# Decoder on one core: TensorE turns the identity matrix into an unread bank at the heads of stages and ahead of the last output projections

## The reference, cut to what matters

```python
x = _layernorm(x + _L0_attn_ref(x, ...))            # 16 heads of 128, rope             -> stage a
x = _layernorm(x + _L0_xattn_ref(x, ctx_1024, ...)) # 32 heads of 16, axial rope        -> stage b
x = _layernorm(x + _L0_ffn_ref(x, ...))             # 32 experts of 80 rows, top 4 of 3 groups, and a shared one
x = _layernorm(x + _L1_attn_ref(x, ...))            # 16 heads of 32, causal            -> stage d
x = _layernorm(x + _L1_xattn_ref(x, ctx_1024, ...)) # 16 heads of 128, rms-normed q, k  -> stage e
x = _layernorm(x + _L1_ffn_ref(x, ...))             # 8 experts, top 2
```

```python
q = x @ Wq; k = s @ Wk; v = s @ Wv        # s is x itself, or the context
w = softmax(q @ k.T * scale)
return (w @ v) @ Wo
```

## Time and profile before

| | us |
|---|---|
| median of 3 runs (lowest, highest) | 3435.64 (3432.76, 3437.16) |
| the profiled execution's own time | 3431.57 |
| its span | 3429.8 |
| PE busy | 3125.4 (91%) |
| DVE busy | 2102.3 (61%) |
| POOL busy | 1478.2 (43%) |
| ACT busy | 1293.4 (38%) |

### The profile page before, as it was taken

One profiled execution on the slowest core, in us unless ns is written; L12 is line 12 of the kernel. 1 busy time (PEld: TensorE's weight loads), 2 busy tenths in 40 slices (PEclk: granted clock), 3 DMA queues, 4 the chain that ended last, 5 costly groups with the idle time before them and its releaser, 6 DMA issues. The chain is left out here.

```text
span 3429.8 us, 58056 instructions
## 1 busy us (share of the span) xinstructions
PE 3125.4 (91%) x20720; PEld 2611.0 (76%) x20720; DVE 2102.3 (61%) x3794; ACT 1293.4 (38%) x3291; POOL 1478.2 (43%) x1470
## 2 busy tenths in 40 slices
PE   7999999999969999899896999699999999969991
PEld 5887878878857777678674777488888888759991
DVE  5666566676636767621185777566667677745566
ACT  3343333333336666401222333244444444324440
POOL 4554343444422343310163222255555556545565
PEclk9999999999989999889997999799999999979996
DMA  4001016022310111149574112210101001147665
GB/s 175 16 13 57 0 36 235 0 79 104 141 48 26 48 34 62 69 164 339 173 166 123 37 40 65 98 60 25 47 12 48 11 24 38 47 172 242 238 228 159
DMA packets 137869, 317.13 MB, mean 92 GB/s; under 512 B 18425, under 2 KB 30457, under 8 KB 135538
## 3 DMA queue, kind: packets, MB, share of 16 engines
q1 hardware_dynamic: 120194, 274.61, 23.7%
q0 software_dynamic: 15360, 36.25, 4.2%
q10 hardware_dynamic: 2160, 4.21, 0.3%
HBM read 231.07 MB, written 98.04 MB: 96 GB/s over the span
## 5 line engine op out<-in xcount | busy, mean ns | idle before, releaser
L398 POOL TENSOR_TENSOR a_sq<-a_tq,a_sinq 128x256 f32<-128x256 f32 x128 | 150.5, 1195 | 357.0 <-DVE a_tq L476 355.7
L398 POOL TENSOR_TENSOR a_sk<-a_tk,a_sink 128x256 f32<-128x256 f32 x128 | 124.0, 988 | 90.0 <-DVE a_tk L476 90.0
L364 ACT COPY a_probT<-bank 128x512 f32<-128x512 f32 x64 | 37.5, 587 | 327.4 <-PE bank L715 327.4
L411 POOL TENSOR_TENSOR e_sk<-e_tk 128x512 f32<-128x512 f32 x64 | 66.5, 1039 | 203.1 <-DVE e_tk L503 203.1
L353 ACT ACTIVATE e_prob<-bank,e_nb,e_rq 128x128 f32<-128x128 f32 x256 | 114.0, 456 | 85.8 <-DVE e_nb L577 85.8
L348 ACT ACTIVATE a_sm<-a_sm,a_nmax 128x128 f32<-128x128 f32 x256 | 99.9, 392 | 121.7 <-DVE a_nmax L572 121.7
L954 ACT ACTIVATE b_prob<-bank,b_nb 128x128 f32<-128x128 f32 x512 | 139.4, 387 | 10.3 <-DVE b_nb L1152 10.3
L1048 POOL TENSOR_TENSOR d_prob<-d_prob,d_nmax 128x1024 f32<-128x1024 f32 x32 | 64.0, 1998 | 183.3 <-DVE d_nmax L1147 183.3
L2482 POOL TENSOR_TENSOR n_wu_lo<-nw_wu,n_wu_hi 128x1408 fp32r<-128x1408 f32 x23 | 74.3, 3231 | 127.2 <-DVE n_wu_hi L2526 127.2
L498 DVE TENSOR_TENSOR a_kr<-a_kr,a_sk 128x512 f32<-128x512 f32 x64 | 66.4, 1037 | 89.1 <-POOL a_sk L398 89.1
L1149 DVE TENSOR_REDUCE b_nmax<-bank 128x8 f32<-128x1024 f32 x64 | 77.7, 1215 | 63.6 <-PE bank L1293 62.8
(11 more groups left out here) (542 smaller groups left out, 10753.5 us busy)
## 6 DMA issues: line engine op xcount, KB each, us to landing
packed<-all_zero SPq DMA_DIRECT2D x32, 1024.0 KB, 8.9
cw_wg<-in_c_wg SPq DMA_DIRECT2D x32, 512.0 KB, 5.2
cw_wu<-in_c_wu SPq DMA_DIRECT2D x32, 512.0 KB, 6.1
cw_wd<-in_c_wd SPq DMA_DIRECT2D x32, 512.0 KB, 8.4
nw_wg<-in_f_wg SPq DMA_DIRECT2D x23, 704.0 KB, 5.6
nw_wu<-in_f_wu SPq DMA_DIRECT2D x23, 704.0 KB, 7.6
nw_wd<-in_f_wd SPq DMA_DIRECT2D x23, 512.0 KB
nw_xe<-packed SPq DMA_DIRECT2D x46, 256.0 KB, 2.7
```

Source lines behind the costliest of these rows:

```text
L364: nc.scalar.copy(probT[:], pP[:, :]).then_inc(act_pt, 1)
L398: step = nc.gpsimd.tensor_tensor(o, i, s, ALU.mult)
```

## The change

A new function puts n transposes of the identity matrix, 128 x 128 in float32, into a PSUM bank that nobody reads at that moment. They wait for nothing and signal nothing. 402 of them go into PE's row, at these places (before and after are seen from the instruction named):

- a: 30 after `turn_x(0)`; 30 in the last slot ahead of the wait for the softmax (`v_p`); 24 ahead of the last output
- b: 20 before and 36 after `turn_x(0)`; 34 ahead of the last output
- capped experts: 12 before `turn_x(0, 0)`
- d: 12 before and 28 after `turn_x(0)`; 42 ahead of the last output but one, 30 ahead of the last
- e: 20 before and 20 after `turn_x(0)`; 30 in the last slot ahead of `v_p` and behind the router's transposes; 24 ahead of the last output
- routed experts: 10 after `turn_x(0, 0)`

In the first block, during the first loads, PE gets nine matmuls of a zero tile of 128 columns, once that tile has been set. No instruction of another engine is added, removed or moved.

```diff
+def keep_busy(nc, bank, tile, n):
+    for _ in range(n):
+        nc.tensor.transpose(bank[:, 0:P], tile[:, 0:P], tile[:, 0:P])
...
@@ wide_attention, slot
+                if last:
+                    keep_busy(nc, pQ, ident, 30)
                 pe.wait_ge(v_p, done(u))
...
@@ wide_attention, around the loop
+            keep_busy(nc, pO, ident, busy[0])
             turn_x(0)
+            keep_busy(nc, pO, ident, busy[1])
             pe.wait_ge(g_lo, done(0))
...
             probs_v(u, 1)
+            keep_busy(nc, pQ, ident, 24)
             output(G - 1, B - 1)
...
@@ narrow_attention, around the loop
+            keep_busy(nc, pP, ident, busy[0])
             turn_x(0)
+            keep_busy(nc, pP, ident, busy[1])
             pe.wait_ge(w_lo["q"], 1)
...
             each_batch(pe, slot)
+            keep_busy(nc, pJ, ident, busy[2])
...
+            keep_busy(nc, pJ, ident, busy[3])
             output(B - 1, (0, 3 * C), False)
...
@@ capped_experts
+            keep_busy(nc, pO[1], ident, 12)
             turn_x(0, 0)
...
@@ routed_experts
             turn_x(0, 0)
+            keep_busy(nc, pO[1], ident, 10)
...
@@ first block
+            @block.tensor
+            def _(pe):
+                pe.wait_ge(g_z, 1)
+                for _ in range(9):
+                    nc.tensor.matmul(psum[7][:, 0:P], zero[:, 0:P], zero[:, 0:P], start=True, stop=True)
...
+ a: busy=(0, 30)   b: busy=(20, 36, 0, 34)   d: busy=(12, 28, 42, 30)   e: busy=(20, 20)
```

More of the change, by code:

```diff
@@ L83, in split_product, with wide_attention @@
     return nc.tensor.matmul(ps, a_hi, b_hi, start=False, stop=stop)
-def wide_attention(nc, name, psum, ident, x_src, x_dst, w_dram, staged, head, rope=None, rms=None, background=None, keep=None, ahead=None, head_ready=False, router=None):
+def wide_attention(nc, name, psum, ident, x_src, x_dst, w_dram, staged, head, rope=None, rms=None, background=None, keep=None, ahead=None, head_ready=False, router=None, busy=(0, 0)):
     G, H = 4, 4
@@ L739, in _, with narrow_attention @@
             probs_v(u, 1)
+            keep_busy(nc, pQ, ident, 24)
             output(G - 1, B - 1)
-def narrow_attention(nc, name, banks, ident, x_src, x_dst, w_dram, NH, plan, staged, head, rope=False, causal=False, keep=None, router=None, ahead=None, head_ready=False):
+def narrow_attention(nc, name, banks, ident, x_src, x_dst, w_dram, NH, plan, staged, head, rope=False, causal=False, keep=None, router=None, ahead=None, head_ready=False, busy=(0, 0, 0, 0)):
     DH = D // NH
@@ L2861, in decoder @@
         wide_attention(nc, "a", psum, ident, x, x1, of("a_"), staged_a, head_a, rope=True, background=zero_rows, ahead=fetch_b,
-                       head_ready=True)
+                       head_ready=True, busy=(0, 30))
         with ExitStack() as moe:
@@ L2868, in decoder @@
             narrow_attention(nc, "b", banks, ident, lambda b: x1[b], None, {**of("b_"), "ctxT": ctxT}, 32,
-                             PLAN_8, staged_b, head_b, rope=True, keep=xall, router=router, ahead=fetch_c, head_ready=True)
+                             PLAN_8, staged_b, head_b, rope=True, keep=xall, router=router, ahead=fetch_c, head_ready=True, busy=(20, 36, 0, 34))
             base, weight = sc.sbuf("base", [P, B, D]), sc.sbuf("weight", [P, B, 4])
@@ L2884, in decoder @@
             combine(nc, "cc", base, result1, router.rows, weight, x2, 4, rest, staged_d.fetch)
-        narrow_attention(nc, "d", banks, ident, lambda b: steps[0][b], lambda b: steps[1][b], of("d_"), 16, PLAN_4, staged_d, head_d, causal=True, ahead=fetch_e)
+        narrow_attention(nc, "d", banks, ident, lambda b: steps[0][b], lambda b: steps[1][b], of("d_"), 16, PLAN_4, staged_d, head_d, causal=True, ahead=fetch_e, busy=(12, 28, 42, 30))
         with ExitStack() as moe:
@@ L2890, in decoder @@
             router = SpreadRouter(nc, sc, tri, ones, ident, xall, w, packed2)
-            wide_attention(nc, "e", psum, ident, x3, None, {**of("e_"), "ctxT": ctxT}, staged_e, head_e, rms=True, keep=xall, router=router)
+            wide_attention(nc, "e", psum, ident, x3, None, {**of("e_"), "ctxT": ctxT}, staged_e, head_e, rms=True, keep=xall, router=router, busy=(20, 20))
             weight, rows = sc.sbuf("weight", [P, B, 2]), sc.sbuf("rows", [P, B, 2], U32)
```

## The result

| | before | after |
|---|---|---|
| median of 6 runs each (us) | 3435.51 | 3423.69 |
| lowest, highest | 3431.18, 3437.27 | 3417.39, 3427.97 |
| profiled execution (span) | 3431.57 (3429.8) | 3424.90 (3423.1) |
| mean granted clock | 0.955 | 0.965 |

The ratio is 0.9967 with an interval of [0.9954, 0.9979]: the change saves 0.33%, 11.8 us by the medians. On another occasion, with 5 runs beside 18 of the kernel before, it was again faster, 0.9962 [0.995, 0.9975]. The forecast was 3421.3, a saving of 14.3. The two profiled executions are only 6.7 apart, and the trace shows where the rest is.

The account below looks back on a forecast made before the run. PE bounds the kernel, at half clock after waits. Ends 13.8, b's head -3.3, d's +1.3, e's -2.0, experts +4.5 sum to 14.3 us less: 3421.3, own range 3410 to 3428, 8-in-10 range 3410 to 3437.

Parts of the forecast that it names:

- The ends: Ends of stages a, b, d, e: seven 12-matmul outputs go from about half to full clock; net saving 13.8 us.
- The first rival: Turns don't hold the clock, so every wait holding turns costs its overrun: 20 us taken, time 3455.6, chance 0.12.
- The second rival: The clock still falls in half of the ends: gain only 1.8 us, time 3433.8, chance 0.14.
- The third rival: Outputs are quicker, but heads and the barrier's DMA wait take up gains: 2.6 us left, about 3433, chance 0.08.
- Head of b: Start of stage b: 20 turns ahead of `turn_x(0)` go at half clock and delay ACT, DVE, PE: costs 3.3 us.
- Head of e: Start of stage e: 20 turns ahead cost 3.3 us, full clock gives back 1.3: net cost 2.0 us.
- Head of d: Start of stage d: 28 turns keep q and k at full clock, v then waits for `d_wv_lo`: saves 1.3 us.
- Capped experts: First experts' 78 matmuls: 12 turns in the wait ahead may avoid half clock; half of 9 taken, saving 4.5 us.
- Routed experts and the first block: Ten turns before a wait of about their length, and nine matmuls under the first loads: 0 us each.

Follow-up runs that it names:

- the ends alone: Changed kernel without the turns at the heads and experts and without the first block's zero matmuls: ratio 0.9955 to the kernel before, median 3417.18 beside 3430.97.
- the kernel without the leading turns: Changed kernel without the 20 turns ahead of the first transposes of b and the 20 of e: ratio 0.9961 to the kernel before the change.

## Why the prediction was right, by its steps

- **The ends: forecast 13.8, measured 13.7**, and 13.6 in the second trace of the change. The seven outputs take 20.4 where 21.0 were worked out. From their first matmul's start to their last's they are 14.5 shorter (14.9 forecast); e's last slot cost 2.0 (2.2 forecast) and gave back 1.14 at the router's matmuls (1.1). This carries the whole result. How steady the overrun is the forecast didn't ask: in two of nine traces it is 3.7.
- **Turns hold the clock.** The first rival is out: in the ten traces with the turns of the ends in their number (one of them with 10 in e's last slot), all 70 outputs ran at 1.00; of the 21 without turns one did. The rule of the Trainium skill, "TensorE: Matmul & The Clock Gate", Part 4 (PE-mode transpose), that the clock does not engage for transposes, is not what these turns show, which are float32 and stand in the trace as plain MATMUL. The second rival is out for the change as it is, and nearly true for half as many turns.
- **The third rival, that the gains are taken up behind the outputs, is out for the ends.** With the ends alone a's end saves 3.79, and the first transposes of b come another 0.2 earlier; the medians show 13.8.
- **Head of b: forecast +3.3, measured +4.2 and +4.4.** The first part has the right path and came out smaller. The first transposes are 3.6 later (4.3 forecast), and ACT's row for the context 2.0, since its wait of 1.00 is gone. So q and v start 2.0 late and not 3.3. The second part the forecast did not have. It took the 36 turns behind the transposes as worth nothing; up to 2.2 came from them, since a quicker q and k leave a pause of 3.1 ahead of v, in which the clock falls. That the sum is near the forecast is luck: one part too high, the other left out. And the second trace of the kernel before adds 1.4 in this head by itself.
- **Head of e: forecast +2.0, measured +1.9 and +2.0** by the second tile. Against the kernel without the leading turns these cost some 3.3 there; that kernel takes off 1.3, but so do traces without any turns in e's head (0 to 1.1), so what the turns behind give back, 1.3 in the forecast, is not shown.
- **Head of d: forecast -1.3, measured -1.3 and -0.5, but not shown to be the turns'.** By d's first v matmul the mechanism shows: the five traces with turns are 1.4 to 2.0 early there, eight without between 0.2 late and 1.2 early, and in four of the five v then waits 0.6 to 0.9 for `d_wv_lo`, as forecast. In the change's first trace it doesn't wait: the clock fell in the middle of q and came back in k. By 1900.14 the gain can't be told any more. Seven traces without turns there took off 0.8 to 1.8 over the same stretch (a second trace of the kernel before: +0.3), five with them 0.5 to 1.9.
- **Capped experts: forecast -4.5, measured -0.3 and -0.2 in the two traces of the change.** Half of 9 was taken for want of knowledge, and no trace has it: each of the 14 has the stretch either in 9.57 or in some 18, and with 12 turns, in five different kernels, three traces of six gain 8.7 to 9.2. So this step failed as the forecast of one execution. Whether it holds as a mean over runs of this kernel is not shown. The 9 itself is borne out (18.44 to 9.57), though the forecast's own 10.6 for 78 would make it 7.8.
- **Routed experts and the first block: nothing**, as said; they weren't tried alone.
- Sum without the experts: 13.7 - 4.2 - 1.9 + 1.3 = 8.9, against 11.8 in the medians; the experts' gain in some of the runs would be one explanation for the difference, which the times alone don't show. The trace's own 6.7 has 2.2 of drifts in it that don't repeat. The forecast of 14.3 is near 11.8 on the strength of the ends; without the experts' 4.5 it would have been 9.8. Its own range is a little off: the terms that it names for the ends give 3411.5 and 3429.1, not 3410 and 3428.

## What to carry to other kernels

At the end of a stage, where one engine is the whole chain and waits for others, dummy work that ends before the wait does is free, and here it brought what comes behind it from half clock to full: count the wait in the timeline, fill nearly all of it, and never overrun it. Half as many turns kept it at four outputs of seven. At the head of a stage leave the engine alone in front of the instruction that others wait for, and look at what the quicker matmuls will wait for next, since a pause that they open can drop the clock again. Where a long dense stretch begins at half clock, look at the pause ahead of it first: with 20 or 28 instructions in it the stretch was 9 us shorter in each of four traces here. And before a stretch of two single traces is called gained or lost, take a second trace of the unchanged kernel: untouched stretches drifted by 2 to 6 us here.

## What was not expected of the hardware

A dense stretch did not by itself bring back the full clock: PE was busy all of the 18.44 us of the first experts' matmuls, at half clock, while b's last output got it back within its 12 matmuls. In the trace before:

```profile
1434.31:1438.45 4.14, 4.14 (x10) 0.50 0.00 0
1438.47:1439.25 0.78, 0.77 (x4) 1.00 0.00 0
```

The same 12 turns in the same place left the experts' first matmuls at full clock in three executions and at half in three others, and an empty rest of 3.52 kept the clock where one of 1.97 lost it. What decides there no run shows.
